# Order of the next pair's projections: query and key by halves in place of both halves of one kind

## The reference

```
latent_kv = x @ w_kv_down                    # 256 -> 128
k, v = split(latent_kv @ w_kv_up)            # 16 heads of 64
q = x @ w_q
att = softmax(where(causal, q k^T * 64**-0.5, -inf))
y = (att v) @ w_out
```

## Time and profile before

| | us |
|---|---|
| median of 3 runs | 1794.89 |
| lowest, highest | 1793.68, 1796.0 |
| the profiled execution's own time | 1797.59 |
| its span, first to last instruction | 1796.3 |
| TensorE busy | 1737.0 |
| VectorE busy | 1250.7 |
| ScalarE busy | 887.7 |
| GpSimdE busy | 854.0 |

### The profile page before, as it was taken

The page is one execution under the profiler, slowest core; times in us unless marked ns, Lnnn a source line. Parts: engine busy times, 40 slices in busy tenths (PEclk is TensorE's granted clock), DMA queues, the critical chain, the costliest instruction groups (busy, mean ns, idle before and its releaser), DMA issues.

```text
span 1796.3 us, 40559 instructions
## 1 busy us (share of the span) xinstructions
PE 1737.0 (97%) x16006; PEld 1207.7 (67%) x16006; DVE 1250.7 (70%) x2766; ACT 887.7 (49%) x1968; POOL 854.0 (48%) x1282
## 2 busy tenths in 40 slices
PE   9999999999999999999999999999999999999998
PEld 5666685668566767566856667756685666766667
DVE  5888848626788885753678887675468888676545
ACT  4676634223577763322457775432246767443233
POOL 2777842221187874241138777314114877731410
PEclk9999999999999999999999999999999999999999
DMA  6555570321255554040135555305013555530500
GB/s 185 129 134 127 125 208 31 54 42 37 69 138 128 128 120 149 1 81 15 37 92 131 130 126 122 133 2 95 0 43 103 134 126 124 132 109 2 94 1 25
DMA packets 119915, 164.42 MB, mean 92 GB/s; under 512 B 30032, under 2 KB 86832, under 8 KB 118704
## 3 DMA queue, kind: packets, MB, share of 16 engines
q1 hardware_dynamic: 105760, 155.03, 35.9%
q10 hardware_dynamic: 13968, 6.82, 1.3%
HBM read 63.16 MB, written 4.24 MB: 38 GB/s over the span
## 4 chain that ended last, share of the span: by engine, by line
PE 72%; DVE 14%; ACT 5%; SPq 4%; DMA 3%; issue 1%; POOL 1%; ACTq 0%; DVEq 0%; POOLq 0%
PE scores L466 13%; PE bank L684 10%; PE scores L664 9%; PE bank L719 4%; PE bank L466 4%; SPq L1002 4%; DVE prob L813 3%; ACT prob L924 2%; PE scores L1776 2%; PE scores L1686 2%; PE scores L1114 2%; DMA placed<-prob 2%; PE bank L725 2%; PE bank L721 2%; PE scores L1748 2%; PE scores L437 2%
## 5 line engine op out<-in xcount | busy, mean ns | idle before, releaser
L882 POOL COPY placed<-prob 32x768 f32<-32x768 f32 x384 | 315.5, 822 | 27.5
L297 POOL TENSOR_TENSOR rstd<-rstd,minus_half 128x2 f32<-128x2 f32 x96 | 69.7, 728 | 533.1 <-DVE rstd L296 531.0
L684 PEld LDWEIGHTS bank<-placed,v_t 128*64 128x64 f32 x4608 | 250.0, 137 | 75.7 <-issue 70.5
L684 PE MATMUL bank<-placed,v_t 128*64 128x128 f32 x4608 | 272.7, 275 | 9.9 <-DMA placed<-hx 4.8
L664 PE MATMUL scores<-k_t,q_t 64*128 64x512 f32 (+3 forms) x1536 | 275.1, 496 | 0.8 <-ACT rec_t L934 0.8
L806 DVE CUSTOM_DVE_ANT_0 mod_rows<-scores,hx 128x128 f32<-128x128 f32 (+7 forms) x256 | 191.8, 749 | 75.5 <-PE scores L664 75.5
L813 DVE STREAM_TRANSPOSE prob<-prob 128x1536 f32<-128x1536 f32 x128 | 222.9, 1765 | 27.4 <-ACT prob L924 27.1
L806 DVE CUSTOM_DVE_ANT_0 x<-scores,hx 128x128 f32<-128x128 f32 (+7 forms) x256 | 192.7, 753 | 0.0
L924 ACT ACTIVATE prob<-mod_rows,neg_max 128x128 f32<-128x128 f32 (+2 forms) x192 | 137.3, 715 | 102.9 <-DVE neg_max L806 86.6
L664 PEld LDWEIGHTS scores<-k_t,q_t 64*128 64x128 f32 x1536 | 129.5, 186 | 85.1 <-issue 62.0
L870 POOL COPY rec_wide<-rec 128x128 f32<-128x128 f32 x256 | 65.0, 289 | 226.6 <-DVE rec L817 168.6
(11 more groups left out here) (249 smaller groups left out, 3435.8 us busy)
## 6 DMA issues: line engine op xcount, KB each, us to landing
placed<-prob SPq DMA_DIRECT2D x640, 96.0 KB, 2.2
f<-in_L_ffn_f SPq DMA_DIRECT2D x16, 2048.0 KB, 13.6
placed<-hx SPq DMA_DIRECT2D x320, 96.0 KB, 2.2
mod_rows<-mod_scratch SPq DMA_DIRECT2D x32, 128.0 KB, 4.3
out<-x SPq DMA_DIRECT2D x16, 256.0 KB, 2.2
w_ring<-in_L_attn_w_q ACTq DMA_DIRECT2D x24, 128.0 KB, 2.6
w_ring<-in_L_attn_w_kv_up ACTq DMA_DIRECT2D x48, 64.0 KB, 2.0
next_x<-in_L_attn_x SPq DMA_DIRECT2D x6, 512.0 KB, 4.1
```

The source lines that it names most:

```text
L297: step = pool.do(lambda e, ts=ts: nc.gpsimd.tensor_tensor(rstd[:, ts], rstd[:, ts], minus_half[:, ts], op=ALU.pow), var, filled)
L684: last = nc.tensor.matmul(out_bank[rows_, at_:at_ + P], v_t[pair % 2][:, j, rows_], placed[m % 2][:, :, head, first_block(m, i) + j, :], s ...
L882: nc.gpsimd.tensor_copy(placed[m % 2][target * GROUP:(target + 1) * GROUP, source, :, :, :], prob[m % 3][source * GROUP:(source + 1) * GRO ...
```

## The change

The jobs of pairs 1 to 7 get an order of their own, q0, k0, q1, k1, v0, v1. With two jobs a round, the first kind of round now has q0 and k0, the second q1 and k1; the third has v0 and v1 as before. Banks go by the place in this order instead of by the half, so the first and the second job of each round keep theirs. Pair 0, which is projected ahead of round 0, keeps its order. The two engines that count jobs, TensorE and ScalarE, count in the new order.

```diff
@@ -537,6 +537,7 @@
         ROUNDS_OF = len(ROUND_TILES)
         ROUNDS = PAIRS * ROUNDS_OF
         JOBS = ("q0", "q1", "k0", "k1", "v0", "v1")
+        NEXT_JOBS = ("q0", "k0", "q1", "k1", "v0", "v1")
         SCORE_BANKS = 3
         Q_SCALE = -(HD0 ** -0.5)
         ROWS_OF = (slice(0, HD0), slice(HD0, P))
@@ -605,18 +606,18 @@
 
         def jobs_of(m):
             pair = m // ROUNDS_OF + 1
-            return [(pair, j) for j in JOBS if round_of(pair, j) == m] if pair < PAIRS else []
+            return [(pair, j) for j in NEXT_JOBS if round_of(pair, j) == m] if pair < PAIRS else []
 
         FILLING = 4
 
         def round_of(pair, j):
-            return ROUNDS_OF * (pair - 1) + (JOBS.index(j) // 2 if (pair, j) != (1, "v0") else 1)
+            return ROUNDS_OF * (pair - 1) + (NEXT_JOBS.index(j) // 2 if (pair, j) != (1, "v0") else 1)
 
         def in_out_bank(pair, j):
-            return int(j[1]) == (0 if pair and round_of(pair, j) < FILLING else 1)
+            return NEXT_JOBS.index(j) % 2 == (0 if round_of(pair, j) < FILLING else 1) if pair else int(j[1]) == 1
 
         def job_number(pair, j):
-            return len(JOBS) * pair + JOBS.index(j) + 1
+            return len(JOBS) * pair + (NEXT_JOBS if pair else JOBS).index(j) + 1
 
         def act_job_number(pair, j):
             return job_number(pair, j) - (2 if pair or j[0] == "v" else 0)
```

## The result

| | us |
|---|---|
| before, median of 10 runs | 1794.3 |
| after, median of 10 runs | 1798.59 |
| ratio, 95% interval | 1.0026, 1.0017 to 1.0035 |
| after, the profiled execution: time, span | 1799.25, 1797.8 |
| the same pair again, in a later comparison: before (33 runs), after (11) | 1796.53, 1798.55 |

The account below looks back on a forecast made before the run. TensorE, busy 97% of the span, was taken as the bound. Batch starts 3.48 plus 0.33 for batch 0, less 3.56 of stalls, gave +0.25 us: 1795.1 on the median 1794.89, range 1791.3 to 1798.9.

Parts of the forecast that it names:

- cost nothing: Mid-batch: rounds of 9.41, 7.89 and 7.76 us become 8.54, 8.76 and 7.76; the pair stays 25.06.
- rival D: Mid-batch, first-to-second-kind edge: VectorE, with 0.31 us left, starts late by 0.2 in 28 pairs; at most +5.6, 1800.7; 5%.
- The stalls go, and don't move to the third kind: Mid-batch: values products stop waiting for second-kind moves; the third kind's margin falls from 1.7 to 0.9 us, no new stall.
- Rival C: Mid-batch: stalls move to the third kind's moves and void the gain; +3.8 us, 1798.7; 15%.
- the sum of 3.56 us over the eight long rounds: Mid-batch: eight first-kind rounds last longer than 9.41 us; each excess should go whole, minus 3.56 us.
- The loss at the batch starts: Rounds 3 and 4: TensorE waits 0.87 us more, then round 4 costs 0.87 more; plus 3.48, and 0.33 in batch 0.
- Rival B: Batch starts: rounds 3 and 4 cost nothing, later waits absorb the 0.87; only the gain remains, 1791.3 us; 10%.
- rival E: Batch starts: half of the 0.87 is won in rounds 0 and 1; 1.7 us less than forecast, 1793.4; 10%.

Follow-up runs that it names:

- experiment 5: The changed kernel run again, unaltered, against the kernel before in the second comparison: ratio 1.0012, median 1798.55 us against 1796.53.
- the filled wait: The changed kernel with k0's product made twice in round 3, result unchanged, against the kernel before: ratio 1.0008.
- the early read: The changed kernel with ScalarE reading q0 of round 3 after four exponentials instead of six, against the kernel before: ratio 0.9996.

## Why the prediction was wrong

- **Mid-batch, "cost nothing": right.** 8.55, 8.76, 7.76, and 25.07 a pair; rival D didn't happen, with 0.31 us left at the edge as worked out.
- **The stalls go, and don't move to the third kind: right in kind.** In four profiles of the changed kernel one second-kind round from round 7 on was long, by 0.08 us. Rival C is out. The rule of the Trainium skill, DMA: Bandwidth & Descriptors, section Issuing engines are not separate DMA queues, would have given C. No run here tests what it says; the third kind's moves kept enough room all the same.
- **The size of that gain was off.** The first step that failed is the sum of 3.56 us over the eight long rounds: it was read from one execution, and four others gave 2.58, 2.06, 1.16 and 2.46. The new order for pairs 3 to 7 alone won 2.2 clock-free. With the mean, 2.4, instead of 3.56, the sum is +1.4 and not +0.25; measured clock-free, it is +1.4 in experiment 5. I had written that the stalls depend on how long single moves take, and then put the one execution's difference on the median all the same.
- **The loss at the batch starts: right.** 3.81 forecast, 3.62 in the profiled pair; the filled wait shows in all four batches, and the early read in batches 1 to 3, that it is the cover over ScalarE's read of q0. Rival B and rival E are out: rounds 0 to 2 together came out even in batches 1 and 2, +0.30 in batch 0 (0.33 forecast).
- **A term was missing, the second step that failed: the clock.** I gave the longer wait of round 3 a price of its own length. In batch 0 it went from 1.23 to 2.10 us, and within the product behind it TensorE fell to half clock, 1.68 us more. I had looked at the clock only in mid-batch, where it was 1.00, and not asked of a lengthened wait what clock follows it.
- **Slips in the sums.** The range ends at 1798.9 where rival C gives 1798.7, and half of rival B's chance is 0.05, not the 0.07 given for faster. Neither changes the forecast. The eight stalls are 3.0 of the wait list's 3.3 us; the rounds are each some 0.07 longer than their wait.

1.4 for the corrected sum and 1.7 for the clock, in the executions that have it, make 3.1. That is inside the second comparison's interval (0.5 to 3.8 us) and at the lower end of the first's (3.1 to 6.3). The first term is shown by the experiments. The second is shown in single executions; in the mean clocks it stands less clearly: 0.9983 over the 21 runs of the changed kernel against 0.9989 over the 74 of the kernel before and its copy, which is 1.1 us, while the clock also falls in other places, and in kernels that don't have the longer wait. The first comparison's median, 4.3, is more than the sum. The changed kernel's clock-free span is alike in both comparisons, 1794.2 and 1794.5, but the kernel before showed 1794.3 us in the first and 1796.4 and 1796.5 in the two later ones. Its clocks in the first aren't on record. Whether its executions had fewer cold stretches there stays open.

## What to carry to other kernels

A job moved out of a round that waits into one that doesn't costs its full length, even where the sum of the work is the same: look for the wait that an engine's order leaves behind the job, and shorten that wait first. A stall read from one execution is a sample; take its size from several before it pays for a certain loss. And a wait made longer on TensorE can have a second price, the clock behind it: look at the granted clock behind every wait of the length that yours will have.

## What the runs showed of the hardware

- Behind a wait of 2.1 us TensorE's clock fell to the lower level in five of seven executions of round 3 in batch 0, behind one of 1.2 us in none of five. The fall began 0.1 to 1.3 us into the product behind the wait and cost 1.6 to 1.7 us each time. With round 22 of batches 0 and 3 it fell behind 10 of 13 waits of 1.96 to 2.10 us, and behind none of 27 of 1.23 to 1.83. This holds for these two places: near 1776 us it fell in one execution behind a wait of 0.99 us.
- The same instructions ran cold near 1776 us in one kernel's execution and warm in another's; mean clocks of one kernel reached from 0.997 to 1.000, and its spans differed by up to 6.5 us, more than any single change here is worth.
- Single moves land after 2.2 us as a rule and after up to 4.1 now and then, and an issue takes 0.6 us as a rule and 1.5 to 2.2 now and then; which rounds stall changes from execution to execution.
